# A decoder layer on one core: the self attention's maximum is subtracted by GpSimd in batches 0 to 4 instead of 0 to 2, with a new plan of the order

## The reference

```
x = x + attn(layernorm(x))              # self attention, 16 heads of 16
x = x + xattn(layernorm(x), ctx, mask)  # cross attention on 375 keys, 16 heads of 16
x = x + ffn(layernorm(x))               # top 2 of 8 experts, gated slot attention
# attn:  scores = (q k) / 4, -inf above the diagonal; softmax(scores) v; then Wo
# ffn:   rms norm, softmax(x Wg), top 2; tokens gathered per expert; k, v, f with
#        the expert's weights; scan in chunks of 64; scattered back, summed, rms norm, Wo
```

## Time and profile before

| what | us |
|---|---|
| median of 3 runs (395.94 to 397.52) | 395.95 |
| the profiled execution, its own time | 397.27 |
| its span, first to last instruction | 395.5 |
| PE busy in the span | 372.8 (94%) |
| DVE busy | 296.0 (75%) |
| ACT busy | 291.6 (74%) |
| POOL busy | 131.8 (33%) |
| granted clock of TensorE, mean | 0.996 |

### The profile page before, as it was taken

The page is one execution under the profiler, slowest core; times in us unless marked ns, Lnnn a source line. Parts: engine busy times, 40 slices in busy tenths (PEclk is TensorE's granted clock), DMA queues, the critical chain, the costliest instruction groups (busy, mean ns, idle before and its releaser), DMA issues.

```text
span 395.5 us, 11330 instructions
## 1 busy us (share of the span) xinstructions
PE 372.8 (94%) x3803; PEld 286.2 (72%) x3803; DVE 296.0 (75%) x1163; ACT 291.6 (74%) x795; POOL 131.8 (33%) x187
## 2 busy tenths in 40 slices
PE   8888999999999999998889689999999999999996
PEld 6776878778777767776666455655668888878885
DVE  3987988897599888766845967466678898698663
ACT  4053897798679979999996758978876666677562
POOL 3667341220321333161311392025053633334320
PEclk9999999999999999999999989999999999999999
DMA  7998963465362321320020335346251312212101
GB/s 192 203 277 275 340 176 88 134 179 167 58 196 92 73 68 43 93 68 16 26 64 2 123 125 181 139 172 215 83 189 44 107 36 73 70 36 84 49 13 58
DMA packets 23079, 45.76 MB, mean 116 GB/s; under 512 B 2776, under 2 KB 14664, under 8 KB 23024
## 3 DMA queue, kind: packets, MB, share of 16 engines
q1 hardware_dynamic: 20976, 37.70, 31.5%
q0 software_dynamic: 2048, 7.34, 6.4%
HBM read 26.69 MB, written 18.35 MB: 114 GB/s over the span
## 4 chain that ended last, share of the span: by engine, by line
PE 65%; DVE 13%; ACT 11%; DMA 5%; issue 4%; SPq 1%; POOL 0%; ACTq 0%; DVEq 0%
PE ps L870 48%; PE ps L873 17%; DVE sc L1279 3%; ACT sc L1618 2%; ACT pT L1626 2%; DMA xbo<-in_x 2%; DMA kv<-kd_d,idk 1%; ACT u L1689 1%; ACT pT L1612 1%; ACT u L1687 1%; DMA kd_d<-kd 1%; DMA xs<-xs_d 1%; ACT u L1691 1%; DVE st L1226 1%; DVE scs L1289 1%
## 5 line engine op out<-in xcount | busy, mean ns | idle before, releaser
L1618 ACT ACTIVATE sc<-sc,nm 112x375 f32<-112x375 f32 x128 | 77.2, 620 | 4.0 <-DVE nm L1279 3.8
L1279 DVE CUSTOM_DVE_ANT_0 sc<-ps,mkb 112x375 f32<-112x375 f32 x128 | 65.2, 542 | 11.1 <-PE ps L870 10.9
L870 PE MATMUL ps<-wm,xsT 128*128 x168 | 59.3, 500 | 1.4 <-DVE kd L1472 0.8
L873 PEld LDWEIGHTS ps<-cst,sc 112*125 112x125 f32 x384 | 47.2, 188 | 10.5 <-issue 4.2
L873 PE MATMUL ps<-cst,sc 112*125 112x112 f32 x384 | 54.4, 280 | 0.5
L1626 ACT ACTIVATE pT<-ps 125x448 f32<-125x448 f32 x96 | 51.5, 558 | 3.3 <-PE ps L873 3.0
L870 PEld LDWEIGHTS ps<-wm,xsT 128*128 128x128 f32 x168 | 31.3, 193 | 24.6 <-issue 22.7
L870 PE MATMUL ps<-cxT,cqT 32*112 32x375 f32 x256 | 28.5, 517 | 2.5 <-DVE nm L1279 1.0
L1289 DVE CUSTOM_DVE_ANT_0 scs<-ps,cst 112x112 f32<-112x112 f32 x128 | 27.3, 267 | 2.7 <-PE ps L873 1.3
L1472 DVE SCALAR_TENSOR_TENSOR kd<-ps,u 128x512 f32<-128x512 f32 x21 | 14.4, 688 | 18.3 <-ACT u L1691 14.0
L1829 POOL DMA_INDIRECT xs_d<-y,idu x16 | 16.2, 1015 | 33.6 <-DVE idu L1378 18.1
(11 more groups left out here) (229 smaller groups left out, 926.5 us busy)
## 6 DMA issues: line engine op xcount, KB each, us to landing
kd_d<-kd SPq DMA_DIRECT2D x21, 384.0 KB
xs_d<-xs SPq DMA_DIRECT2D x8, 896.0 KB, 8.6
wm<-in_wmoe SPq DMA_DIRECT2D x8, 768.0 KB, 5.0
cxp<-in_ctx SPq DMA_DIRECT2D x8, 420.4 KB
cxT<-in_ctxT SPq DMA_DIRECT2D x32, 93.8 KB, 3.7
xs<-xs_d SPq DMA_DIRECT2D x21, 128.0 KB, 2.0
mki<-in_mask SPq DMA_DIRECT2D x8, 164.1 KB, 6.3
out<-xbo SPq DMA_DIRECT2D x8, 112.0 KB, 1.9
```

The source lines that it names most:

```text
L870: return e.matmul(o, l, r, start=start, stop=stop)
L873: return e.transpose(o, i, ident[0:n, 0:n])
L1279: e.tensor_tensor_reduce(sc[:, m % RS, j, :], ps[0:S, bk, 0:NK], mkb[:, b % 2, :], 1.0, 3e38, ALU.add, ALU.min, nm[:, m % RS, j:j + 1]).th ...
L1618: e.activation(sc[:, n % RS, j, :], sc[:, n % RS, j, :], ACT.Exp, bias=nm[:, n % RS, j:j + 1], scale=-1.0).then_inc(a_ex, 1)
```

## The change

`PSB` goes from 3 to 5. With it the two `sb` stages of each unit of batches 3 and 4 run on POOL; PE's wait in front of their transposes changes from the semaphore of DVE to that of POOL, since both places use `PSB`. The arithmetic is the same. All five tables of `BIAS` have new numbers, so that the order on every engine is another one; the source of the tables is two lines shorter, so that line 1296 of the kernel before is line 1294 of the changed one, and so on.

```diff
@@ -40,7 +40,7 @@
 HW = 17 * 16 + 15
 NH = 2 * NB
 N_TB = 6
-PSB = 3
+PSB = 5
 LATE, SP0 = 3, 24.0
 WARM = ()
@@ -110,31 +110,29 @@
 BIAS = {
-    "T": {"G": 2152, "R": -1395.2, "Sc": -316.9, "Ss": -8083.7, "at": 25.6, "cnt": -214.1, "combine0": -1243.9,
...
+    "T": {"G": 1411.9, "R": 1494.2, "Sc": -1299, "Ss": -3275.8, "at": 132.7, "cb": 184, "cnt": -7513,
...
```

More of the change, by code:

```diff
@@ L112 @@
 BIAS = {
[4 rows of a table removed]
-          "pkf": -5089, "pvc": 1024.3, "pvs": 6856.2, "pvx": 74.1, "qTx": 3617.4, "qgT": 87.4, "qk": 197.9,
-          "regs": 26.8, "siT": 2830.6, "sta": -1398, "stx": 2468.8, "tm": -20, "tpc": 613.1, "tqs": -1226.1,
[6 rows of a table removed]
[L125 to L128, removed]
-    "A": {"cpc": 2278.4, "cross_q": 1528.1, "dec": -449.3, "dre": -133.7, "e": 1445.1, "es": 2146.9,
-          "exc": 1302.6, "fT": 2518.2, "fs": 146.1, "kTx": -45.4, "oTc": -31.8, "oTs": -79.3, "onT0": -596.7,
[5 rows of a table removed]
-    "S": {"gx": 959.8, "kd": -23.4, "late": 194.9, "later": -301, "ldctxT": -508.6, "ldmask": 139.2,
-          "zero": 566.6},
[4 rows of a table added]
+          "pb": -198.2, "pkf": -445.7, "pvc": 1299.3, "pvs": -28.7, "pvx": 1465.5, "qTx": 2910, "qk": -15.5,
+          "regs": 1052.6, "siT": 2455.2, "sta": -6.7, "stx": 1269.2, "tm": 1332.5, "tpc": -219.9, "tqs": -12.3,
[6 rows of a table added]
+          "rwa": 2827.1, "rwb": 109.7, "si": 205.5, "slots": -339.7, "split": -987.1, "stats0": -48.7,
+          "stats1": 681.8, "stats2": 26.9, "tb0": 176.7, "tb1": 1716.7, "tb2": 1491.4, "tb3": -138.8,
+          "tb4": 98.5, "tb5": -6.1, "tm": 157.4, "top": 70.5, "v": -711.9, "xn0": 5477.6, "xn1": 841.8,
+          "y": -429.8},
+    "A": {"cpc": 6579.5, "cross_q": -46.3, "dec": 344.2, "dre": -2060.4, "es": 4525.3, "exc": 997.6, "fT": 29,
+          "fs": 106, "kTx": 816.3, "oTc": -5455.3, "oTs": 935.3, "onT1": 426.9, "ones": 29.1, "q": -66.1,
+          "qTx": 1676.5, "qe": 958.6, "qgT": -192.6, "qx": 176.1, "siT": 4878.1, "sig": -264.3, "sp": -166.9,
[3 rows of a table added]
+    "S": {"gx": 185.9, "late": 163.5, "later": -7.2, "ldctx": 10.9, "ldctxT": 52.3, "out": 6.5, "zero": 150.3},
 }
```

## The result

| | before | changed |
|---|---|---|
| median of 4 runs each, us | 396.47 (395.94 to 397.52) | 391.90 (390.65 to 392.05) |
| profiled execution: own time, span | 397.27, 395.5 | 391.83, 390.0 |

The ratio is 0.9886, 95% interval 0.9861 to 0.9911: 4.5 us, 1.1%, faster. The forecast said faster by 2.3 us with a range of 390.0 to 398.5; the sign and the range held, the size was half. The terms behind it did worse than the sum, as the stretches show.

What follows compares the result with a forecast made beforehand. PE was taken to bound the kernel nearly everywhere, with only its 22.7 us of waits to win back. Terms -1.5 - 1.6 - 0.4 + 1.2 = -2.3 us took the 395.95 us median to 393.7, range 390.0 to 398.5.

Steps and rivals of the forecast that it cites:

- The crowded stretch of DVE: Cross batch 3: DVE's load falls, so PE's waits on DVE shrink; -1.5 us, bounds -3.6 and +1.5.
- the crowd only moves: Rival: cross batch 2 gets almost as full on DVE, and both main gains are near 0; 396.8 us, chance 0.26.
- The batches 4 to 7 keep their shares of ACT, and ACT limits them as before: nothing there.: Later attention batches: ACT is the limiting engine and stays so; no gain claimed.
- The subtraction itself: Batches 3 and 4: moving eight `sb` from DVE to POOL costs 0, as PE has other transposes to do.
- From attention to experts: Between batch 7's `oproj` and tile 3: earlier `cnt` and loads bring tile 3 sooner; -1.6 us, bounds -3.5 and +1.
- about 16: Sign between attention and experts: tile 3's first matmul about 16 us behind batch 7's `oproj` start instead of 17.3.
- The idle time ahead of `yT`: Between attention and experts: PE newly idles about 2.2 us, as batch 7's `yT` needs `y`.
- The first gather: PE's 0.50 us wait for `kv`: `kTx`, needing only the first gather, takes its place; -0.4 us, from -0.5 to 0.
- Changes of mode: PE's whole list: eight more places where the array changes mode, 180 against 172; +1.2 us, from 0.8 to 1.8.
- POOL's queue holds PE: Rival, batches 3 and 4: subtractions queue behind POOL's mask waits and reach PE late; up to 399.2 us, chance 0.17.
- The engines get in each other's way: Rival: each of the eight subtractions costs DVE or PE 0.35 us by contention with POOL; 396.5 us, chance 0.05.

Runs made afterwards that it cites:

- the middle experiment: Changed kernel with the stages within cross batches 2 and 3 in the old kernel's relative order: 400.65 us, ratio 1.0121.
- the end experiment: Changed kernel with the stages within cross batches 5 to 7 in the old kernel's relative order: 392.92 us, ratio 0.992.
- the old order's other trace: Kernel before with only the eight subtractions of batches 3 and 4 moved from DVE to POOL: 397.08 us, ratio 1.003.
- the same kernel's second trace: Changed kernel run again with no edit, against the kernel before: 392.81 us, ratio 0.9861.
- the second try: Changed kernel with tile 0's expert matmuls right behind its transposes, batch 7's count behind both first tiles' matmuls: 395.01 us, ratio 0.9983.
- the third: Changed kernel with stages between attention and experts moved once more, plus four unread matmuls ahead of the first `pkf`: 393.31 us, ratio 0.9945.

## Why the prediction came out as it did

- **The crowded stretch of DVE, -1.5 (bounds -3.6 and +1.5).** Right in place and sign, and the middle experiment bears it out. Cross batches 3 and 4 lost all 2.41 us of PE's idle time, while cross batch 2, whose DVE rose to 24.36 of 28.0 us between 76.8 and 104.8 and not to 27, got no new waits. The term was under-sized by about 1 us; the rival *the crowd only moves* fell. Two readings under it were off. The 2.5 us of waits on DVE in batch 3 added waits of the weight loads to waits of the matmuls, which are partly the same gaps; PE's count had 1.3 us idle there. And DVE fell to 20.50 us, not 18, of a stretch that became shorter itself, so that its share stayed at 91%: full by that measure, and yet PE waits for nothing.
- **"The batches 4 to 7 keep their shares of ACT, and ACT limits them as before: nothing there."** This is the step that failed most. ACT was busy for 54.46 of 56.55 us before, and the stretch then took 53.08 with 52.84 busy. By the share only 2.1 us could go; 3.5 went, though at most about 0.8 of them by work that moved (one exponential and one copy fewer in the stretch, one `xnT` more). ACT's instructions overlap in the record (51.69 + 0.61 lies behind 52.20, the start of the next one), and the sum of their durations is 71 us in both stretches: the share counts latency, and it was no limit. (The Trainium skill, Perfetto Trace Analysis, Identifying the Most-Contended Engine, takes the occupancy of ScalarE also as a fair measure of how close it is to roofline; in this stretch the measurement differs from it: 3.5 us came off where the share left 2.1.) Before, ACT itself waited for PE there, 1.8 us in its rows, and in the changed kernel not at all; PE's loads waited for DVE as much as for ACT, and it is the waits on DVE that fell most: `nm` from 3.9 us to 0.9, all on DVE from 5.3 to 2.2, those on ACT from 4.7 to 3.5. PE's own idle time fell by 1.5 us and its busy time by 2.0, the latter partly work moved into the stretches ahead. So the prediction named one engine and looked no further. Over the whole attention the loads' waits on ACT fell by 8.2 us, on DVE by 5.7, and those on issue rose by 6.6; I had the fall on ACT at 0. The rows don't say how many us of the end each is worth; the end experiment shows that 1.3 of the 3.5 us are the order inside.
- **The subtraction itself, 0.** Its consumers were covered, as argued. What stood behind them in DVE's queue was not: left on DVE, batch 3's four cost 1.8 us by way of a cross maximum, ACT's queue and `cqT`. (The stages of batches 3 and 4 lie between 42 and 72 us; the 92 in the prediction takes in batch 5.) The prediction asked who waits for the subtraction; it should have asked what stands behind it.
- **From attention to experts, -1.6.** Tile 3 starts 20.1 us behind `oproj`, against 17.3 before and 16.7 forecast (the prediction's "about 16" among its signs is this 16.7). Of those 2.8 us, about 1.1 are `pb` and a `qTx`, done ahead, and 0.6 the two `x` that stood ahead of `oproj` before, so 1.1 are lost. The idle time ahead of `yT` was forecast at 2.2 and is 2.1. Behind it the granted clock is 0.50, which costs 2.6 us more, and this no term contained; it is most of the 3.4 us by which the forecast was missed. The rows showed before's own instance, 0.97 over that stretch. The unread matmuls show that the clock is at work: with it kept up, the place takes 18.3 us. But before paid too, only later: 3.4 us at the lower clock reach from just ahead of tile 3 into its matmuls. From tile 3 to the end it is 163.2 instead of 165.85: 1.1 of that is the `pb` and `qTx` already done, and about 13.35 x 0.09 = 1.2 is the lower clock (0.91 from 229.65 to 243.0, now 1.00 at that place). So by the start of tile 3 the term has the wrong sign, from `oproj` to the end it is nothing in the profiled pair (183.1 and 183.3), and against the old order's other trace, with 6.8 us at the lower clock as well, it is -1.5. With two traces of the old order, what it is worth in the medians stays open.
- **The first gather, -0.4.** The wait of the earlier trace rows is gone.
- **Changes of mode, +1.2.** Neither right nor wrong as a sum: waits of weight loads that end in issue rose by 6.6 us over the attention, but a wait that an engine ended before may now be listed as issue. The rows don't separate the two.
- **POOL's queue holds PE:** refuted, also with all 32 stages there: the largest wait of PE for POOL was 0.8 us. POOL's wait for the masks fell from 26.7 us to 14.6 on DVE and 1.0 on PE.
- **The engines get in each other's way:** small. The twelve subtractions left on DVE take 713 ns, 73 more than before; 12 x 0.073 = 0.9 us on an engine with room. Three of them run beside an `xn` of POOL and take 0.90 to 1.09 us, the other nine 0.62; before, one of 20 did (the 0.99 of the earlier trace rows). The Trainium skill (GPSIMD Engine Reference, Specifications) names contention of GpSimd with DVE instructions that have two SBUF inputs, over the interfaces that they share; the three pairs agree with it. The `xn` beside them kept their 0.73 us, so POOL did not pay here. With the eight subtractions back on DVE the same three take as long, so it is the new order that makes the pairs, not the move.

That the sum came within its range was partly luck: in the profiled pair a missed gain in the attention (5.7 instead of 1.5) was offset by a gain behind it that did not show, and the two largest causes, PE's waits in the batches given to ACT and the lower clock behind a gap, were in no term.

## What to carry to other kernels

An engine's busy share says neither that it limits nor that it doesn't: sum what the weight loads (or the bounding engine) wait for, by releaser and by stretch, and take the share only where that sum agrees. When a stage leaves a full in-order queue, follow what stands behind it there, through the next queues, until the bounding engine waits; an order planned for the stage's old place did not use the room here. Gaps of 2 us in all in PE's work ahead of large matmuls cost more than their length; price them by the granted clock of such places. A few unread matmuls in them paid for themselves here. And before a stage's cost is read from one pair of traces, compare how long each spent at the lower clock, and look for a second trace of the same order: two traces of one order differed by 1.4 us in a stretch here.

## What was not expected of the hardware

With PE busy for 0.64 of 2.4 us, and no single gap above 1.2 us, the granted clock fell to 0.50 for the next 6.8 us, and the four `wm,xsT` matmuls of a `pkf` took 3.67 us instead of 1.9. In the same kernel's second trace it fell later, 1.6 us behind the second gap, and stayed down for 3.4 us. The same was seen in other orders: among 4.2 us of gaps in the second try (four matmuls then took 3.78 us), among 2.7 us in the third (3.77 us), and for 3.4 us behind the joint's wait of 2.35 us in the middle of the attention. Nine unread 128x128 matmuls in the gaps kept it at 1.00, and the kernel became 2.2 us faster for doing more.
